# The second expert bias of two expert layers: from one product per group of tiles to one product behind the loop

## The reference

```python
probs = softmax(x @ Wr + br)                    # 16 experts
topk_w, topk_idx = top_k(probs, 2)
topk_w = topk_w / topk_w.sum(-1, keepdims=True)
h = einsum('nc,ech->neh', x, W1) + b1
h = gelu(layernorm(h, g1, be1))
expert_out = einsum('neh,eho->neo', h, W2) + b2 # b2: the second expert bias
y = sum(take(expert_out, topk_idx) * topk_w)    # x = x + 0.5 * y
```

## Time and profile before

| What | Value |
|---|---|
| median of 3 runs | 693.43 us |
| profiled execution: span from the first to the last instruction | 603.3 us |
| outside the span (median less span) | 90.1 us |
| PE busy | 495.1 us, 82% of the span |
| DVE busy | 461.9 us, 77% |
| ACT busy | 313.2 us, 52% |
| POOL busy | 164.0 us, 27% |
| mean granted TensorE clock | 0.914 of full speed |
| L1285, the product with the bias rows | 32 instructions, 385 ns each (median) |

### The profile page before, as it was taken

How to read it: one execution, slowest core, us unless ns; L and a number is a source line. 1 busy time by engine, 2 the same in 40 slices (tenths; PEclk the granted TensorE clock), 3 DMA queues, 4 the chain that set the end, 5 groups by cost and what they waited for, 6 DMA issues and landing times.

```text
span 603.3 us, 9389 instructions
## 1 busy us (share of the span) xinstructions
PE 495.1 (82%) x3064; PEld 269.9 (45%) x3072; DVE 461.9 (77%) x1226; ACT 313.2 (52%) x613; POOL 164.0 (27%) x206
## 2 busy tenths in 40 slices
PE   6786989999999999899787899597896787799800
PEld 3452422222222222244365788485654454688600
DVE  4988898988878987465897889668877766978822
ACT  2354456777776678687142677444341101567700
POOL 5020030010000110001374604672101074711765
PEclk8898999999999999999888899878897888899955
DMA  6006400049705003000326295411000015273532
GB/s 208 3 6 162 90 2 0 21 110 193 247 2 141 3 9 63 2 1 1 118 87 166 81 310 152 135 36 28 1 0 1 2 52 140 76 221 88 156 104 65
DMA packets 55773, 49.48 MB, mean 82 GB/s; under 512 B 5406, under 2 KB 47918, under 8 KB 55342
## 3 DMA queue, kind: packets, MB, share of 16 engines
q1 hardware_dynamic: 34974, 31.21, 19.3%
q0 software_dynamic: 4368, 9.54, 5.9%
q10 hardware_dynamic: 16384, 8.13, 4.8%
HBM read 25.90 MB, written 20.60 MB: 77 GB/s over the span
## 4 chain that ended last, share of the span: by engine, by line
PE 48%; DVE 26%; POOL 8%; issue 7%; ACT 6%; DMA 3%; SPq 0%; POOLq 0%; ACTq 0%; DVEq 0%
PE ps L819 9%; DVE arena L867 8%; PE ps L809 7%; PE ps L766 7%; POOL arena L1198 5%; PE ps L1287 3%; PE ps L1260 3%; POOL rows_in L1171 2%; PE ps L1586 2%; ACT arena L1357 2%; PE ps L207 1%; PE ps L1243 1%; PE ps L1270 1%; PE ps L1642 1%; DMA row<-in_rows 1%
## 5 line engine op out<-in xcount | busy, mean ns | idle before, releaser
L867 DVE TENSOR_REDUCE arena<-ps 128x1 f32<-128x1024 f32 x128 | 150.8, 1219 | 25.1 <-PE ps L766 24.8
L932 ACT ACTIVATE arena<-ps 128x512 f32<-128x512 f32 x256 | 138.4, 602 | 55.2 <-PE ps L809 52.9
L809 PE MATMUL ps<-arena 99*128 99x512 bf16 x256 | 85.5, 383 | 1.2 <-ACT arena L932 1.0
L766 PE MATMUL ps<-arena 96*128 96x512 bf16 x256 | 76.6, 381 | 7.0 <-DVE arena L867 6.7
L1198 POOL DMA_INDIRECT arena<-rows_out,route x64 | 61.2, 957 | 68.9 <-DMA rows_out<-arena 47.7
L1171 POOL DMA_INDIRECT rows_in<-xl,route x64 | 62.5, 977 | 53.3 <-DVE route L1123 35.1
L819 PE MATMUL ps<-arena 128*32 128x512 f32 x512 | 68.2, 605 | 1.9 <-ACT arena L928 1.3
L809 PEld LDWEIGHTS ps<-arena 99*128 99x128 bf16 x256 | 22.3, 97 | 73.0 <-ACT arena L932 48.8
L254 POOL TENSOR_TENSOR small<-small,nhalf 128x8 f32<-128x8 f32 x11 | 18.2, 1656 | 121.3 <-DVE small L276 121.3
L1357 ACT ACTIVATE arena<-ps,route 128x128 f32<-128x128 f32 x124 | 46.4, 461 | 5.2 <-PE ps L1270 5.1
L207 PE MATMUL ps<-zerob 128*128 128x512 bf16 x140 | 41.3, 446 | 2.5 <-POOL zerob L2101 1.4
(11 more groups left out here) (280 smaller groups left out, 825.9 us busy)
## 6 DMA issues: line engine op xcount, KB each, us to landing
arena<-rows_in SPq DMA_DIRECT2D x28, 256.0 KB, 4.3
rows_out<-arena ACTq DMA_DIRECT2D x28, 256.0 KB, 2.9
rows_in<-zerob SPq DMA_DIRECT2D x2, 1920.0 KB, 11.0
arena<-att_parts SPq DMA_DIRECT2D x12, 256.0 KB, 8.7
arena<-in_consts SPq DMA_DIRECT2D x2, 1024.0 KB, 6.7
arena<-zerob SPq DMA_DIRECT2D x1, 2048.0 KB, 10.1
arena<-att_parts SPq DMA_DIRECT2D x14, 128.0 KB, 8.1
att_parts<-arena SPq DMA_DIRECT2D x6, 256.0 KB
```

The costliest lines, as they stand in the source:

```text
L766: ins = pe.matmul(ps[:, bank + keys, :], a_qs[0:96, b, h, j * P:(j + 1) * P], a_ks[0:96, b, h, keys * 512:(keys + 1) * 512], start=True, s ...
L809: pe.matmul(ps[:, score_bank(n), :], a_ks[0:99, b, h0 + h4, i * P:(i + 1) * P], a_qs[0:99, b, h0 + h4, half * 512:(half + 1) * 512], start ...
L867: nc.vector.tensor_reduce(a_nm[:, o % 2, k:k + 1], ps[:, bank:bank + 2, :].rearrange("p a b -> p (a b)"), AX.X, ALU.max, negate=True).then ...
L932: nc.scalar.activation(a_p[:, n % 16, :], ps[:, score_bank(n), :], ACT.Exp, scale=0.25).then_inc(a.ex, 1)
```

## The change

`b2` leaves the loop. The product L1285 and all that fed it go: the constants `tile` and `pick` and their cast on POOL, the three small DVE steps in `moe_vector_slots`, the split of `b2`, its store, four indirect gathers and twelve spreading DMAs. The `w2` products open their own sums.

In its place a table `b2d` of 128 by 8 by 128 (f32) is laid out once: POOL clears it and SP fills it with eight DMAs, so that rows 16 j to 16 j + 15 of block j hold `b2`. Behind each loop two new functions run. On DVE, `moe_vector_b2` scales the one-hot rows of both halves by the gates, in place, and adds first and second expert; PE turns the two results (`moe_tensor_b2`), DVE copies them to SBUF, PE multiplies them with `b2d` in four f32 products of 512 columns, and DVE adds the four results to `x`. Only then does DVE add the gathered rows. In code:

```diff
@@ moe_vector_slots
-            yield vs.mark(nc.vector.tensor_scalar(r_te[0:32], r_base[0:32, 1:1 + NE], cc("tile")[0:32], None, ALU.is_le))
-            yield vs.mark(nc.vector.tensor_reduce(r_tc[0:32], r_te[0:32], AX.X, ALU.add))
-            nc.vector.tensor_scalar(r_tix[b][0:32], r_tc[0:32], NE - 1.0, None, ALU.min).then_inc(m.tix, 1)
@@ moe_pool_send
-                if k == m.b:
-                    moe_pool_bias(pool, m)
@@ moe_sync
-                    if g == (0, 4)[m.b]:
-                        moe_sync_bias(sp, m)
@@ moe_tensor, out(u)
-                if g == 0:
-                    pe.wait_ge(m.brow, 48 * m.turn)
-                pe.matmul(ps[:, bank, :], pick[:, g, :], brow[:, m.b, :, :], start=True, stop=False)
                 for j in range(k):
                     ins = pe.matmul(ps[:, bank, j * P:(j + 1) * P], t_a[:, u % 2, j * P:(j + 1) * P],
-                                    w2[...][:, bass.ds(at[j], P)], start=False, stop=(j == k - 1))
+                                    w2[...][:, bass.ds(at[j], P)], start=True, stop=True)
@@ new
+        def moe_tensor_b2(pe, pair):
+            pe.wait_ge(Moe.gw, pair[1].i + 1)
+            pe.wait_ge(s_b2d, 16 * TB)
+            for m in pair:
+                ins = pe.transpose(ps[:, TURN_IN_BANKS[0], m.b * P:(m.b + 1) * P], r_oh[m.b][:, 0].rearrange("p t e -> p (t e)"), cc("ident"))
+            ins.then_inc(Moe.gwt, 1)
+            pe.wait_ge(Moe.gwc, pair[1].i // B + 1)
+            for m in pair:
+                for q in range(2):
+                    ins = pe.matmul(ps[:, HIDDEN_BANKS[2 * m.b + q], :], r_gt[:, m.b, :], b2d[:, 4 * q:4 * q + 4, :], start=True, stop=True)
+            ins.then_inc(Moe.gb, 1)
+
+        def moe_vector_b2(dve, vs, pair):
+            for m in pair:
+                dve.wait_ge(m.gate, m.i + 1)
+                for k in range(2):
+                    ins = nc.vector.tensor_tensor(r_oh[m.b][:, k], r_oh[m.b][:, k], bc(r_e[m.b][:, k, :].unsqueeze(2), [P, TB, NE]), ALU.mult)
+                vs.step(ins)
+                nc.vector.tensor_tensor(r_oh[m.b][:, 0], r_oh[m.b][:, 0], r_oh[m.b][:, 1], ALU.add).then_inc(Moe.gw, 1)
+            turn = pair[1].i // B + 1
+            dve.wait_ge(Moe.gwt, turn)
+            nc.vector.tensor_copy(r_gt[:, :, :], ps[:, TURN_IN_BANKS[0], 0:B * P].rearrange(...)).then_inc(Moe.gwc, 1)
+            dve.wait_ge(Moe.gb, turn)
+            for q in range(2 * B):
+                xq = x[:, 4 * q:4 * q + 4, :]
+                ins = nc.vector.tensor_tensor(xq, xq, ps[:, HIDDEN_BANKS[q], :].rearrange(...), ALU.add)
+            vs.step(ins)
@@ sync
-            sp.dma_start(bias_parts, b2p[:, :, :]).then_inc(s_b2row, 16)
+            sp.wait_ge(s_b2z, 1)
+            for j in range(TB):
+                sp.dma_start(b2d[NE * j:NE * (j + 1), j, :], A["b2"]).then_inc(s_b2d, 16)
@@ bias_rows
-            steps.step(nc.gpsimd.tensor_copy(b2p[:, 0, :], b2[:, :]))
-            ...
+            nc.gpsimd.memset(b2d[:, :, :], 0.0).then_inc(s_b2z, 1)
@@ gpsimd, at the start
-            nc.gpsimd.tensor_copy(pick[:, :, :], bc(cc("pick")[0:24].unsqueeze(2), [24, 8, P])).then_inc(s_set, 1)
@@ vector, behind the loops (m3 and m5 alike)
             def behind_m3():
+                moe_vector_b2(dve, vs, m3)
                 moe_vector_add(dve, vs, m3[0])
@@ tensor, behind the loops (m3 and m5 alike)
             moe_tensor(pe, m3, between_m3)
+            moe_tensor_b2(pe, m3)
```

More of the change, by code:

```diff
@@ L44 @@
 _at = 0
-for _name, _n in (("ident", P), ("causal", P), ("blocks", P), ("rank", NE), ("quarter", 4), ("ones", P), ("head", NH), ("tiles", 32), ("tile", 1), ("pick", 8)):
+for _name, _n in (("ident", P), ("causal", P), ("blocks", P), ("rank", NE), ("quarter", 4), ("ones", P), ("head", NH), ("tiles", 32)):
     CCOLS[_name] = (_at, _n)
@@ L78, in build @@
         b1r = sb("b1r", [NE, P])
-        b2 = sb("b2", [NE, P])
-        b2r = sb("b2r", [NE, P])
-        b2p = sb("b2p", [NE, 3, P], BF16)
-        brow = sb("brow", [24, B, 4, P], BF16)
-        pick = sb("pick", [24, 8, P], BF16)
+        b2d = sb("b2d", [P, TB, P])
         bo3 = sb("bo3", [96, P], BF16)
@@ L990, in build @@
         r_end = arena_f(19520, 32, NE)
-        r_bias = arena_b(20032, 3, P)
-        r_tix = [route_f(1692 + b, 1).bitcast(I32) for b in range(B)]
-        r_te = route_f(1694, NE)
-        r_tc = route_f(1710, 1)
+        r_gt = route_f(0, B, P)
         t_xg = arena_f(0, B, NGR, 4, P)
@@ L1016, in build @@
             turned, pick = sem("e_bases_turned"), sem("e_tile_one_hot")
-            tix = sem("e_tile_experts")
-            got, rows_got = [sem(f"e_bias_rows{b}") for b in range(B)], [sem(f"e_bias_rows_in{b}") for b in range(B)]
+            gw, gwt, gwc, gb = sem("e_gate_rows"), sem("e_gate_rows_turned"), sem("e_gate_rows_in"), sem("e_b2_by_gates")
             gs, gsel = sem("e_scales_summed"), sem("e_scales_in")
@@ L1025, in __init__ @@
                 self.logit_bank, self.count_bank = banks
-                self.sent, self.bias, self.brow = self.rows_sent[b], self.got[b], self.rows_got[b]
-                self.turn = i // B + 1
+                self.sent = self.rows_sent[b]
                 self.all_sent = 16 * 2 * TB * (i // B + 1)
@@ L1173, in moe_pool_send @@
                         in_=xl[:, TB * b + j, :], in_offset=None).then_inc(m.sent, 16)
-                if k == m.b:
-                    moe_pool_bias(pool, m)
-        def moe_pool_bias(pool, m):
-            pool.wait_ge(m.tix, m.i + 1)
-            pool.wait_ge(s_b2row, 16)
-            if m.i:
-                pool.wait_ge(Moe.rows_got[1 - m.b], 48 * ((m.i - 1) // B + 1))
-            pool.indirect_dma_start(out=r_bias[0:32].rearrange("p i f -> p (i f)"), out_offset=None,
-                                    in_=bias_parts.rearrange("e i f -> e (i f)"),
-                                    in_offset=bass.IndirectOffsetOnAxis(ap=r_tix[m.b][0:32], axis=0)).then_inc(m.bias, 16)
         def moe_pool_fetch(pool, m, ahead_of={}):
@@ L1211, in moe_sync_load @@
                          rows_in[b].rearrange("(j p) c -> p j c", p=P)[:, 4 * g:4 * g + k, :]).then_inc(t.xg[g], 16)
-        def moe_sync_bias(sp, m):
-            sp.wait_ge(m.bias, 16 * m.turn)
-            for i in range(3):
-                sp.dma_start(brow[8 * i:8 * i + 8, m.b, :, :], r_bias[0:32, i, :]).then_inc(m.brow, 16)
         def moe_scalar_store(act, m, g):
@@ L1329, in moe_tensor @@
             out(last - 1)
+        def moe_tensor_b2(pe, pair):
[18 more added lines that the diff above has]
+            dve.wait_ge(Moe.gwt, turn)
+            nc.vector.tensor_copy(r_gt[:, :, :], ps[:, TURN_IN_BANKS[0], 0:B * P].rearrange("p (b t) -> p b t", b=B)).then_inc(Moe.gwc, 1)
+            dve.wait_ge(Moe.gb, turn)
+            for q in range(2 * B):
+                xq = x[:, 4 * q:4 * q + 4, :]
+                ins = nc.vector.tensor_tensor(xq, xq, ps[:, HIDDEN_BANKS[q], :].rearrange("p (a b) -> p a b", a=4), ALU.add)
+            vs.step(ins)
         def turn_bank(left):
@@ L2308, in behind_m5 @@
             def behind_m5():
+                moe_vector_b2(dve, vs, m5)
                 moe_vector_add(dve, vs, m5[0])
@@ L2457, in _ @@
             moe_tensor(pe, m5, between_m5)
+            moe_tensor_b2(pe, m5)
 def shape_constants(np):
@@ L2483, in shape_constants @@
     put("tiles", P * np.arange(32)[None, :])
-    put("tile", P * i[:, None])
-    put("pick", i[:, None] % 8 == np.arange(8)[None, :])
     return c
```

34 lines of the change are left out of this document (14 added, 20 removed).

## The result

The kernel after took 696.86 us in the median of 20 runs (691.27 to 702.09), the kernel before, measured beside it, 694.64 in the median of 20 (692.25 to 699.16). The ratio is 1.0028, with a 95% interval of 1.0014 to 1.0041: 1.9 us (0.28%) slower, inside the 0.3% that counts as no change here (the two medians lie 2.2 apart). The forecast was 692.1 with a range of 689.0 to 696.0; 696.86 lies outside.

The account below looks back on a forecast made before the run. No engine owns the kernel; PE, ACT and DVE are nearly level in the loops and POOL's gathers set the end. Terms -0.95 + 3.35 - 1.0 - 2.7 = -1.3 us gave 692.1, range 689.0 to 696.0.

Parts of the forecast that it names:

- I keep that 90.1: Whole kernel: the 90.1 us between the profiled span, 603.3, and the median, 693.43, was added unchanged to the forecast span.
- The middle: From the linear attention's last first-half turn to the second loop's first hidden product: 1.0 us won, at the second routing.
- Start, -0.95: Kernel start: POOL's cast of `pick` goes, so PE starts at about 12.0, 0.95 us won.
- First loop, PE's end -3.05: First loop: without the extra product and entrance steps, PE's last output product ends 3.05 us earlier, at 381.9.
- Behind the first loop, +3.35: Behind the first loop: the serial block makes PE start the linear attention at 394.15 instead of 390.79, 3.35 us later.
- The rival of products at half clock: Block behind the first loop: its four products take 7.3 us instead of 3.65, time 695.7; chance 0.08.
- that rival: Block's six DVE operations each queue behind a POOL gather on the shared port: up to +4.8 us, 696.9; chance 0.03.
- Second routing, -1.0: Second routing: without POOL's bias gather and three small DVE steps, the chain wins 1.0 us.
- Second loop, -2.7: Second loop: earlier stores let POOL's second half of gathers start 2.7 us earlier; the block stays hidden.
- the rival with 1.8: Behind the second loop: POOL's unexplained wait before its second-half gathers goes, 1.8 us less, 690.3; chance 0.10.
- PE paces the loop alone: Both loops: PE alone limits, eighth store 3.0 us earlier in each, -4.15 in all, 689.3; chance 0.13.
- The loop gives nothing but its ends; slower: Both loops: ACT's work fills the period, eighth store moves only 0.45 us; +2.3 in all, 695.7; chance 0.20.

Follow-up runs that it names:

- d1: The kernel before, unchanged, profiled on a slow chip: 0.9990 (691.7 us), span 689.7.
- b1: The kernel after, unchanged, on a slow chip: 0.9977 of the kernel before.
- b2: The kernel after with the block behind the second loop alone (first mixture's bias missing), on a slow chip: 0.9808 of the kernel before.
- e1: The kernel after, unchanged, on another slow chip (kernel before 695.1 us): 1.0017 of the kernel before.
- b4: The kernel before with the loop's product L1285 taken out and nothing else (bias missing), on a slow chip: 0.9936 of the kernel before.
- c2: The kernel after, unchanged, on a quick chip: 0.9982 of the kernel before, span 605.9.
- f1: The kernel before, unchanged, profiled beside the kernel after on a quick chip: 1.0006.
- f2: The kernel after, unchanged, on a quick chip: 1.0004 of the kernel before.
- c: A job on one quick chip that ran the kernel before (1.0003) and the kernel after (0.9982), among others.
- c1: The kernel before, unchanged, profiled on a quick chip: 1.0003, span 603.3.
- f: A job on another quick chip that ran the kernel before (1.0006) and the kernel after (1.0004).
- e2: The kernel after with DVE's order behind the loop changed and the first half's gathers held until the pair's last store landed, slow chip: 0.9954 of the kernel before.
- a3: The kernel after with a product of zeros put back ahead of each group's output products, on a quick chip: 1.0080 of the kernel before.
- d2: The kernel after with POOL's first-half gathers held until the pair's last store landed, in both loops, slow chip: 0.9938 of the kernel before.

## Why the prediction was wrong

**The step that failed is its first: "the median of the runs, 693.43, lies 90.1 above it, and I keep that 90.1."** The profile was of the quick kind, the times of a slow chip, and a sum made on the one was added to the other. 1.8 us lie outside a span. The forecast missed the time by 4.8 us. Of these 1.2 are no effect of the change: the kernel before has 694.64 in 20 runs where three gave 693.43. The other 3.6 are the change, +2.2 between the medians where -1.3 was forecast. On the slow chips three terms have another size:

- *The block behind the first loop.* The forecast let 3.35 through, since the wait for the first half's last gathers covered the rest. There POOL begins the last of these gathers 17.4 us (d1) and 14.6 us (b1) before PE's last output product ends; d1 turns at once and b1's quarters wait for nothing. No cover is left, and 11.3 us stand open (12.95 less 1.7). b2 beside b1 measures 11.7. The kernel after has the same 12.95 in the first measurement's profile. This is the largest term that was mis-sized, and the only one against the change.
- *The loops* give 3.5 and 4.0 from d1 to b1, against 3.05 and 2.7 to 2.95, but only 0.5 and 1.4 from d1 to e1.
- *The middle* gives 5.1 in one pair of profiles (138.0 to 132.9). The forecast had 1.0 there; b4 has 134.3 with the bias gathers still in, and e1 has 136.6, so most of that is how the waits fell.

The spans of d1 and b1 differ by 3.1 us in all, two chips; the ratio on b1's own chip says 1.6. So there the gains outweigh even the open block. Why two chips gave +1.9 and +1.2 where a third gave -1.6 stays open: on those two it would take loops that give less, as in e1, and no profile of before shows it. The range had no rival in which the gathers no longer cover the block, though 88 unexplained us in a time of 693 left room for any wait. It also stood on three runs of the kernel before.

**By its own steps,** on the quick chips, where they can be tried. The forecast of -1.3 us meets -1.1 (0.9982) and +0.2 (1.0004) there. That is no confirmation: both intervals hold 1.000 as well as the forecast, and the terms missed in both directions.

*Start, -0.95:* the step came and was lost. PE's first product after the fill starts at 11.88 in c2 and 11.69 in the kernel after, where the earlier trace rows has 12.96; the forecast said 12.0. But the first large DVE step of the routing, at 294.32 in the earlier trace rows, is in the kernel after

```profile
294.36 0.68 DVE L1110 TENSOR_TENSOR route<-route 128x128 f32<-128x128 f32 x2
```

On the quick chips it is the same: 12.66 and 11.48 at the start, 294.77 and 294.76 at the routing (f1, f2); in c the routing even comes 0.6 later (295.69, 296.30). The attention between them takes the 1.2 us back.

*First loop, PE's end -3.05:* it was -1.8 (386.4 in c1, 384.6 in c2) and -1.3 (384.3 in f1, 383.0 in f2). DVE's end came 1.35 earlier and not 2.0 (c). Against its own loop's start the last store came 1.15 (c) and 0.7 us (f) earlier, which the forecast itself had named as a sign of being wrong (less than 2), and the eighth store 0.3 earlier in c and 0.2 later in f (from the start of the span 1.0 and 0.4 earlier, where 2.3 was forecast). The gain of the loop's first half is lost at the change of halves. c1 and c2 there:

```profile
351.55 0.42 PEld L1243 LDWEIGHTS ps<-cst,arena 128*128 128x128 f32 x4 [0.27 <-DMA arena<-rows_in]
...
354.25 0.50 DVE L1406 BATCH_NORM_STATS2 arena<-ps 128x6 f32<-128x128 f32 x2 [1.50 <-PE ps L1260]
```

```profile
347.67 5.59 SPq L1185 DMA_DIRECT2D arena<-rows_in  x8
...
350.67 0.66 PE L1211 MATMUL ps<-cst,arena 128*128 128x128 f32 x4 [2.26 <-DMA arena<-rows_in]
...
353.37 0.89 DVE L1401 BATCH_NORM_STATS2 arena<-ps 128x6 f32<-128x128 f32 x4 [1.91 <-PE ps L1228]
```

And f1 and f2:

```profile
349.47 0.66 PE L1243 MATMUL ps<-cst,arena 128*128 128x128 f32 x4 [0.93 <-DMA arena<-rows_in]
```

```profile
348.99 0.66 PE L1211 MATMUL ps<-cst,arena 128*128 128x128 f32 x4 [0.50 <-DMA arena<-rows_in]
```

In all four PE's turn is released by the second half's rows, which SP can load only when POOL's last send has landed, and it starts 25.8 and 25.6 us (c1, c2) and 25.0 and 25.1 us (f1, f2) after the loop's first hidden product, with or without L1285. PE's own wait there says less: it grew from 0.27 to 2.26 in the one pair and shrank from 0.93 to 0.50 in the other. I had expected DVE's wait there (1.30 in the first profile) to shrink by 0.45; it grew by 0.41 (c) and 0.19 (f, 1.27 to 1.46). The engine that I had not asked was POOL: what I read as a wait for PE's products had the sends behind it. No run moved the sends alone.

*Behind the first loop, +3.35:* the working of the block holds. From PE's end to DVE's last quarter it gave 12.2 (381.9 to 394.1), and c2 has 11.8. But PE's end came less early than forecast, so the last turns start 4.0 (c) and 4.8 us (f) later than in the kernel before. The rival of products at half clock came in no run of the kernel after, only in e2. The rule of the Trainium skill on the port that DVE and GpSimd share ("SBUF — State Buffer", section "SBUF: two separate sides") would have put each scaling behind a gather of 0.95 us. In c2 two scalings beside the gather at 381.00 took 0.48 together:

```profile
381.00 0.94 POOL L1173 DMA_INDIRECT arena<-rows_out,route  x1 [0.30 <-issue]
381.08 0.48 DVE L1314 TENSOR_TENSOR route<-route 128x128 f32<-128x128 f32 x2
```

No queueing for a whole instruction is seen. (The sum of that rival, six times 0.97 less 0.8, is 5.0 and not 4.8.)

*SP's eight loads of b2* took 4.24 us (186.7 to 190.95 in c2) and SP next had work at 201.67: hidden, as forecast.

*Second routing, -1.0:* not to be told from the middles of single profiles, which differ by 3 us within one kernel.

*Second loop, -2.7:* it was -3.2 (61.8 to 58.6, c1 to c2) and -1.7 (60.3 to 58.6, f1 to f2), with the tail as before. The size is right, by luck: the path is another. POOL's first 16 gathers were to start 2.4 earlier; against the loop's first hidden product they start at 44.95 in c1 and 44.4 in c2, 43.4 in f1 and 44.4 in f2. What came instead is the rival with 1.8, and more: the 3.1 us before POOL's second half (2.99 in the earlier trace rows) that nothing explained are 0.30 in c2 and f2, and the second row of gathers follows the first at once.

*The rivals:* "PE paces the loop alone" fell with a3. "The loop gives nothing but its ends; slower" named nearly the right time, 695.7, and its half on the first loop is nearer than the forecast's: an eighth store that hardly moves and 1.4 at PE's end, where 1.8 and 1.3 were measured. But it put that on ACT, and on the quick chips the second loop gave 3.2 and 1.7 where it had 0.75. "Nothing measurable" can't be told from the forecast on the quick chips.

## What to carry to other kernels

Before a forecast is made against a measured time, the span of the profile has to be held against it. Here a gap of 13% meant that the two were not the same kind of execution, and every cover read from the profile ("hidden under the gathers") was then an assumption. A block put behind a loop is best ordered so that its products run under work that does not need it, whichever engine is late: the order quarters, sums, last quarter won 1.1% on both kinds of chip where the plain block won 0.2% at most. And a wait that ends with an engine's result may belong to that engine's own wait for data one step earlier. A total that comes out right says little while its terms are not looked up one by one.

## What the hardware showed

On three of the chips the same program takes 85 to 90 us longer, in profiles nearly all of it behind 294 us, where POOL issues indirect DMAs in rows of 16. POOL keeps its pace (0.95 us each and 0.30 between), while PE, DVE and ACT stand for 4 to 12 us at a time, DVE behind products that PE had ended 7.3 us before. With one row of gathers moved behind the loop, the waits in the loop's second half were gone (d2). PE's clock is a part of it and not the whole: from the first hidden product on PE is busy 207 us in c1 and 223 in d1, at a mean granted clock of 0.97 and 0.78 in the first loop, 16 us of some 80. What makes the waits is open. One hint: the trace of c2 has 6833 semaphore increments, that of b1, the same program, only 5013, and of the 1820 lost 759 are landings of POOL's sends and 731 of its gathers. So the names of releasers in the slow traces are less sure; the start times do not rest on them. The Trainium skill ("NOTIFIC — the notification-queue block", section "Overflow: three behaviours, one of which stalls the engine") says that the block that records events can drop records or hold back the engines that produce them. Either could fit; no run here tried it.
